# Three orders in a one-core transformer kernel: eight transposes four units later, a down projection that waits for its input tile by tile, and one row sum ahead of four masked maxima

## The reference

```
x = x + causal_attention(layernorm(x))           # 16 heads of 16, with bias
h = layernorm(x)                                  # input of the block below
for l in range(2):                                # the part the change touches
    q, k, v = split(shift_token(h) @ wqkv[l])     # 8 heads of 64
    q, k = rotary(l2norm(q) * qs, l2norm(k) * ks)
    o = local_attention(8 * q, k, v)              # windows of 128, and the one before
    h = h + o @ wo[l]
    t = layernorm(shift_token(h)) * g + b
    a, g2 = split(t @ w1[l] + b1)                 # hidden size 682 each
    h = h + (a * gelu(g2)) @ w2[l] + b2
x = x + h
```

## Time and profile before

| what | us |
|---|---|
| three runs | 2157.47, 2158.35, 2159.66 |
| their median | 2158.35 |
| the profiled execution, its own time | 2157.21 |
| span of its trace | 2155.4 |
| PE busy in the span | 1973.2 (92%) |
| DVE, ACT and POOL busy | 1466.5, 1260.7, 756.0 |

### The profile page before, as it was taken

The page is one execution under the profiler, slowest core; times in us unless marked ns, Lnnn a source line. Parts: engine busy times, 40 slices in busy tenths (PEclk is TensorE's granted clock), DMA queues, the critical chain, the costliest instruction groups (busy, mean ns, idle before and its releaser), DMA issues.

```text
span 2155.4 us, 36296 instructions
## 1 busy us (share of the span) xinstructions
PE 1973.2 (92%) x12096; PEld 1247.4 (58%) x12096; DVE 1466.5 (68%) x3928; ACT 1260.7 (58%) x3012; POOL 756.0 (35%) x631
## 2 busy tenths in 40 slices
PE   7978999999897669999999999999999999999998
PEld 4522333333234446777777676676777677777766
DVE  7778888888863557568568567557757756856854
ACT  4526666666664337647547646645755764754763
POOL 1033121121322456056046136236515605614610
PEclk9969999999999879999999999999999999999999
DMA  6667534535315620000000000023001000000000
GB/s 182 165 115 148 68 47 61 69 53 93 72 59 144 183 83 1 21 20 1 21 15 6 21 11 11 4 78 113 2 20 40 2 21 30 11 21 21 21 1 30
DMA packets 105335, 112.21 MB, mean 52 GB/s; under 512 B 49772, under 2 KB 84160, under 8 KB 104128
## 3 DMA queue, kind: packets, MB, share of 16 engines
q1 hardware_dynamic: 104576, 100.97, 20.6%
q0 software_dynamic: 576, 8.91, 1.1%
HBM read 67.12 MB, written 42.47 MB: 51 GB/s over the span
## 4 chain that ended last, share of the span: by engine, by line
PE 47%; DVE 6%; ACT 5%; issue 3%; POOL 3%; DVEq 0%; ACTq 0%; POOLq 0%
PE qkv_ps L1368 11%; PE s_ps L1414 5%; PE pt_ps L1485 5%; PE s_ps L1472 4%; PE o_ps L1510 3%; PE qkv_ps L1430 3%; PE pt_ps L1555 3%; POOL inv_norm L1833 2%; PE o_ps L1472 2%; PE pt_ps L1472 2%; PE s_ps L1430 2%; PE o_ps L1555 2%; ACT x_all L1680 2%; PE turn_ps L1394 2%; PE turn_ps L1494 1%
## 5 line engine op out<-in xcount | busy, mean ns | idle before, releaser
L689 ACT ACTIVATE probs<-st_ps 128x512 f32<-128x512 f32 (+3 forms) x768 | 330.0, 495 | 165.5 <-PE st_ps L594 164.9
L1368 PE MATMUL qkv_ps<-w_qkv,x_parts 128*128 128x512 f32 x1152 | 311.8, 415 | 25.6 <-DVE x_all L1925 18.8
L579 PE MATMUL s_ps<-k_stack,q_stack 96*128 96x512 bf16 (+3 forms) x768 | 242.6, 347 | 36.5 <-DVE piece_negmax L734 25.6
L734 DVE CUSTOM_DVE_ANT_0 att_in<-s_ps,causal 128x128 f32<-128x128 f32 (+3 forms) x512 | 233.7, 484 | 42.1 <-PE s_ps L579 41.9
L1368 PEld LDWEIGHTS qkv_ps<-w_qkv,x_parts 128*128 128x128 f32 x1152 | 214.3, 195 | 79.9 <-issue 30.0
L1680 ACT ACTIVATE x_all<-x_all,negmax 128x256 f32<-128x256 f32 (+1 forms) x512 | 249.4, 491 | 8.2 <-DVE negmax L1948 7.8
L1948 DVE CUSTOM_DVE_ANT_0 x_all<-s_ps,band 128x256 f32<-128x256 f32 (+1 forms) x512 | 178.3, 402 | 110.5 <-PE s_ps L1414 110.0
L594 PE MATMUL st_ps<-q_stack,k_stack 98*128 98x512 bf16 (+3 forms) x768 | 241.2, 335 | 12.3 <-ACT probs L689 10.1
L1702 ACT COPY att_in<-pt_ps 128x512 f32<-128x512 f32 (+1 forms) x256 | 143.0, 559 | 147.3 <-PE pt_ps L1485 145.9
L816 POOL TENSOR_SCALAR_AFFINE_SELECT probs<-probs 128x512 f32<-128x512 f32 x128 | 81.2, 634 | 414.7 <-ACT probs L689 414.7
L1841 POOL TENSOR_TENSOR x_all<-x_all,turn_by 128x512 f32<-128x512 f32 x128 | 179.9, 1425 | 101.4 <-PE turn_ps L1394 56.4
(11 more groups left out here) (148 smaller groups left out, 3410.6 us busy)
## 6 DMA issues: line engine op xcount, KB each, us to landing
qk_scratch<-parts SPq DMA_DIRECT2D x64, 192.0 KB, 2.8
q_stack<-qk_scratch SPq DMA_DIRECT2D x96, 128.0 KB, 6.5
k_stack<-qk_scratch SPq DMA_DIRECT2D x96, 128.0 KB, 7.0
w_ffn<-ffn_weights POOLq DMA_DIRECT2D x4, 2176.0 KB, 11.5
x_in<-xt_scratch SPq DMA_DIRECT2D x16, 512.0 KB, 4.1
ffn_weights<-w_high SPq DMA_DIRECT2D x2, 2176.0 KB, 7.5
ffn_weights<-w_raw SPq DMA_DIRECT2D x2, 2176.0 KB, 13.1
att_scratch<-att SPq DMA_DIRECT2D x32, 128.0 KB, 2.0
```

The costliest lines, as they stand in the source:

```text
L579: pe.matmul(s_ps[i % 3][:, 0:kw], q_stack[0:STK, slot, h, qt * P:(qt + 1) * P], k_stack[0:STK, slot, h, k0:k0 + kw], start=True, stop=True ...
L689: act.activation(probs[:, n % 3, h, q0:CH], st_ps[i % 3][:, q0:CH], ACT.Exp).then_inc(exp_done.sem, 1)
L734: dve.tensor_tensor_reduce(seen[:, i % 3, 0:kw], s_ps[i % 3][:, 0:kw], causal[:, CH - kw:CH], -1.0, BIG, ALU.add, ALU.min, result).then_in ...
L1368: mm = pe.matmul(qkv_ps[:, part * CH:(part + 1) * CH], x_parts[:, w % XR, xp, k, :], w_qkv[:, wp, k, part * INNER:(part + 1) * INNER], sta ...
```

## The change

Three edits, all to the written order or to waits; no arithmetic is added or taken away.

```diff
@@ PE, attention part, loop over units u @@
                     if EARLY <= u < UNITS and u % 2 == 0:
                         scores(it, u // 2)
+                    if u == UNITS + 1:
+                        features_first(it, 0)
                     if 2 <= u < UNITS + 2:
                         turn_probs(u - 2)
...
                     if u == NORM_AT:
                         tokens_first(it, 0)
-                    if u == NORM_AT + 5:
-                        features_first(it, 0)
@@ PE, feed-forward part @@
                 def down(c, m):
 
-                    pe.wait_ge(hidden_split.sem, hidden_split.of(it, (c + 1) * HT - 2))
+                    pe.wait_ge(hidden_ready.sem, hidden_ready.of(it, c * HT + HT - 2 - c))
+                    pe.wait_ge(hidden_split.sem, hidden_split.of(it, (c + 1) * HT - 3))
                     steps = [(j, w, h) for j in range(HT) for w, h in PARTS]
                     for n, (j, w, h) in enumerate(steps):
                         rows = P if j < HT - 1 else HL
-                        if n == (HT - 1) * len(PARTS):
-                            pe.wait_ge(hidden_split.sem, hidden_split.of(it, (c + 1) * HT - 1))
+                        if j >= HT - 2 and n == j * len(PARTS):
+                            pe.wait_ge(hidden_split.sem, hidden_split.of(it, c * HT + j))
@@ DVE, end of the feed-forward part @@
                 low(1, HT - 1)
                 if more:
+                    sums(it + 1, 2)
                     mask_scores(it + 1, 0)
                     mask_scores(it + 1, 1)
-                    sums(it + 1, 2)
                 output(1, 0)
```

## The result

The changed kernel took 2165.93 us (median of six, 2161.48 to 2168.56), the kernel before beside it 2158.66 (median of six). The ratio is 1.0031, 95% interval 1.0020 to 1.0042: 4 to 9 us slower. The prediction was 2159.9, with a range of 2154.0 to 2163.5 and no measurable difference the likeliest, so it was wrong. The profiled execution, the slowest of the six, took 2168.56 us against 2157.21 before. Of these 11.35 us some 3.8 had come up by the first token transposes (L1440) of the second half, at 867.21 us against 863.43, in stages that the edits don't touch; 7.6 us came up behind them.

The account below looks back on a forecast made before the run. PE, busy 92% of the span, was taken as the bound, through its holes. -3.6 - 2.75 + 7.9 = +1.55 us on 2157.21 gave 2158.8; the median's 1.14 more made 2159.9 us, range 2154.0 to 2163.5.

Parts of the forecast that it names:

- Edit 1: End of the attention part: moving eight token transposes from in front of the scores gains 0.45 us a pass, -3.6 us.
- Rival 2: Spread sums: the hole comes back in full, Edit 1 gives nothing; +5.2 us, 2163.5 us, slower; chance 0.17.
- Edit 2: First down projection: finer waits let it start sooner, 0.35 us kept in six passes; -2.75 us with passes 3 and 7.
- the last pass's 1.09 us: Pass 7, second half's down projection: its 1.09 us wait goes, starting 1.09 to 1.31 us sooner; pass 7 in all -1.95 us.
- the clock's fall: Pass 3: after 4.9 us idle, low clock on the last three down matmuls and the projection, +1.3 us, bounds 0 and 2.
- Edit 3: End of a pass: a sum ahead of the maxima delays table load and PE's turn of k by 1.13 us; +7.9 us.
- Rival 1: Table load starts by itself, so the delay of Edit 3 doesn't reach PE; -6.35 us, 2152.0 us, faster; chance 0.15.
- rival 3: Thin stretches: shifts move where low clock falls, about 1.3 us each, either direction; 0.08 for results outside the other cases.

## Why the prediction was wrong

**Edit 1** (-0.45 us a pass, bounds 0.34 and 0.57): the mechanism held, and 0.38 was measured between the same transposes in pass 1 (9.06 to 8.68 us), 8 x 0.38 = -3.0. The hole comes back in two pieces, 0.45 us at the scores and 0.31 us at the spread sums, where I had 0.34 (1044.36 to 1044.7) and 0.57. From PE being free to the spread sums it is 2.48 us, as forecast (1051.45 to 1053.93, and 1044.36 to 1046.84), so what is short of 0.45 is the price of the transposes at their new place: about 1.0 us, not 0.91. Rival 2 is wrong for the place. The time of the edit alone, 1.0000, doesn't show the gain.

**Edit 2**: 0.38 us in pass 1, as forecast (0.35), limited by hn_t as forecast; the last pass's 1.09 us is gone. In pass 3 the clock's fall was called, with 1.3 us for it; it costs 7.75 - 5.42 = 2.3, since half clock lasts into the projection for 3.7 us. In sum -2.3 - 1.95 + 2.3 = -1.95, instead of -2.75. (The bounds of that sum come out at -4.3 and -1.8 by its own terms, not -4.4 and -1.7; nothing hangs on it.)

**Edit 3** (+7.9 us): the wait went from 0.33 to 1.48 us in pass 1 and 7.9 us in sum. This term was exact, and so was the reason for it: the load that waits. Rival 1 is wrong.

**The step that failed** is rival 3: the clock "costs or gives about 1.3 us as above, in either direction", so that it only widened the range, by too little. It isn't symmetric at the wait that edit 3 makes longer: there are no falls behind the short wait that could be given back (none in 63 passes with at most 0.49 us idle), and nine in 21 behind the long one (1.45 us or more). I had used this very mechanism in pass 3, for 4.9 us idle, and not asked it of the 1.46 us that edit 3 makes seven times. The trace before had the sign even at this length, at window 4's projection in passes 1 and 2, behind the same wait:

```profile
1141.40 1.63 PE L1368 MATMUL qkv_ps<-w_qkv,x_parts 128*128 128x512 f32 x6 [1.41 <-DVE x_all L1925]
...
1311.48 2.90 PE L1368 MATMUL qkv_ps<-w_qkv,x_parts 128*128 128x512 f32 x6 [1.40 <-DVE x_all L1925]
```

The second has half clock for most of its time, 1.27 us more for the same six matmuls. Asked at edit 3's wait at half the passes and 1.4 us (both taken from the runs, after the fact) it gives +4.9; the profile has 5.0. Beside this 5.0 the other two misses are small: 0.6 us in edit 1 and 0.8 us in edit 2. The corrected sum is -3.0 - 1.95 + 7.9 + 5.0 = +8.0 us, the two measurements of the changed kernel +6.7 and +9.3.

The Trainium skill, TensorE: Matmul & The Clock Gate, has a case that I should have weighed, in the section "A second HAM failure mode: psum-queue depth-cycling": in another kernel frequent short idle times between groups of matmuls made the gate oscillate. This trace agrees in so far as 1.61 us of idle beside short matmuls was followed by half clock in seven of nine passes, in three executions.

## What to carry to other kernels

When an edit lengthens a wait of TensorE that stands in a thin stretch (transposes, short matmuls), price not only the wait but half clock on the large matmuls behind it: here 5 us on top of 8. Put real matmuls into such a wait; if there are none, even useless ones can pay. And before something is put ahead of a scalar engine's first function of another table, look at what releases the table load; one tiny activation ahead can take the load off the path.

## What the runs showed of the hardware

- 35 matmuls of 512 columns more made the kernel 6 us faster, twice.
- Falls came in 2 of 12 passes behind 1.45 to 1.48 us of idle and in 7 of 9 behind 1.61, in three executions.
- At window 4's projection, over all 14 profiles, the first six matmuls took over 2 us instead of 1.63 in 13 of 42 passes behind 0.88 to 0.90 us of idle, in 22 of 42 behind 1.40 to 1.52, and in all 14 behind 1.66 to 2.11 (pass 3).
- An exponential's table load inherits the wait of its exponential: 1.39 us in front of it after the third edit, none ahead of a constant.
- PE's busy time at half clock in the second half is 10 to 31 us over the 14 profiles, which is 5 to 15 us of time. A saved 3 us can drown in that. Which passes have a fall at the projection of window 4 differs from kernel to kernel, and no run here tells why.
